# Condition and bias products moved, transposes at two maxima, last block in chunks, warm rows removed: an adaptive-norm, attention and quantized FFN kernel

## The reference, cut to what matters

```python
def _L0_cond_ref(Efou, y, weight):
    w = scale * weight[:, :, :, 0] * y[:, None, :]
    w = w * jax.lax.rsqrt(jnp.sum(w * w, axis=2, keepdims=True) + 1e-08)
    ...
def _L0_ffn_ref(x, weight, aux_weight1, aux_weight2, bias):
    return jnp.tanh(((x @ weight) @ aux_weight1) @ aux_weight2 + bias)
def _L1_cond_ref(X1, X2, Wq1, bq1, Wq2, bq2, Wk1, bk1, Wk2, bk2, Wv, bv, alpha):
    Q1 = X1e @ Wq1 + bq1; K1 = X1e @ Wk1 + bk1       # X1e: the condition, the same for every token
    Q2 = X2 @ Wq2 + bq2;  K2 = X2 @ Wk2 + bk2
    A = softmax(Q2 K2^T * s) - alpha * softmax(Q1 K1^T * s)
    return A @ (concat(X1e, X2) @ Wv + bv)
def _L1_ffn_ref(x, clip_x, clip_down, w_gate, w_up, w_down):
    xq = _act_fake_quant(x, clip_x[0])               # scale from max(abs(x)) over the tensor
    h = _act_fake_quant(silu(xq @ q(w_gate).T) * (xq @ q(w_up).T), clip_down[0])
    return h @ q(w_down).T
x = x + _L0_ffn_ref(_L0_cond_ref(x, cond, ...), ...)
x = x + _L1_ffn_ref(_L1_cond_ref(cond, x, ...), ...)
```

## Time and profile before

| | |
|---|---|
| median of 3 runs | 229.44 us (228.91 to 229.47) |
| the profiled execution | 227.23 us |
| its span, first to last instruction | 225.4 us |
| granted PE clock, mean | 0.995 of full |
| busy: PE / DVE / ACT / POOL | 214.4 / 161.2 / 121.3 / 109.3 us |
| the chain that ended last | PE 86%, DVE 9%, POOL 1%, ACT 1%, issue 1% |

### The profile page before, as it was taken

One profiled execution on the slowest core, in us unless ns is written; L12 is line 12 of the kernel. 1 busy time (PEld: TensorE's weight loads), 2 busy tenths in 40 slices (PEclk: granted clock), 3 DMA queues, 4 the chain that ended last, 5 costly groups with the idle time before them and its releaser, 6 DMA issues.

```text
span 225.4 us, 4018 instructions
## 1 busy us (share of the span) xinstructions
PE 214.4 (95%) x1556; PEld 185.9 (82%) x1559; DVE 161.2 (71%) x327; ACT 121.3 (54%) x203; POOL 109.3 (48%) x126
## 2 busy tenths in 40 slices
PE   6799999999999999999999999999999899998991
PEld 5699899889999999999999999999999444452480
DVE  1634435899488569688696876958676879998964
ACT  3447824655044919144181541906329889885870
POOL 8240841244000626229377383784951145683782
PEclk9999999999999999999999999999999999999998
DMA  6980008500000000000000000000000000000045
GB/s 188 330 319 7 0 3 236 174 0 3 0 0 3 0 0 3 0 3 1 1 3 0 0 3 0 0 3 0 3 0 0 1 3 1 0 3 0 0 164 208
DMA packets 6970, 9.37 MB, mean 42 GB/s; under 512 B 788, under 2 KB 4904, under 8 KB 6952
## 3 DMA queue, kind: packets, MB, share of 16 engines
q1 hardware_dynamic: 6480, 8.85, 11.6%
q10 hardware_dynamic: 152, 0.26, 0.3%
q0 software_dynamic: 320, 0.01, 0.1%
HBM read 7.02 MB, written 2.10 MB: 40 GB/s over the span
## 4 chain that ended last, share of the span: by engine, by line
PE 86%; DVE 9%; POOL 1%; issue 1%; ACT 1%; POOLq 0%; DVEq 0%
PE ps L1137 57%; PE ps L1509 8%; PE ps L1351 3%; PE ps L1121 2%; PE ps L1592 2%; PE ps L1403 2%; DVE hmax L935 2%; PE ps L1170 1%; PE ps L1575 1%; DVE downT L786 1%; PE ps L1188 1%; PE ps L1316 1%; DVE hi L996 1%; PE ps L1210 1%; PE ps L1614 1%
## 5 line engine op out<-in xcount | busy, mean ns | idle before, releaser
L505 ACT ACTIVATE prob<-prob 128x512 f32<-128x512 f32 x32 | 19.8, 620 | 35.5 <-DVE prob L809 35.5
L1070 POOL TENSOR_TENSOR ptl<-prob,pth 128x512 fp32r<-128x512 f32 x16 | 20.3, 1295 | 37.9 <-ACT pth L417 37.9
L1137 PE MATMUL ps<-xh,x1h 128*128 128x256 f32 x128 | 37.2, 290 | 0.0
L1137 PE MATMUL ps<-xh,x1l 128*128 128x256 f32 x128 | 36.1, 282 | 0.0
L1137 PE MATMUL ps<-xl,x1h 128*128 128x256 f32 x128 | 36.1, 282 | 0.0
L1137 PE MATMUL ps<-vh,ptl 128*128 128x258 f32 x112 | 31.7, 283 | 0.0
L786 DVE TENSOR_REDUCE downT<-ps 128x256 f32<-128x1024 f32 x16 | 19.5, 1217 | 12.3 <-PE ps L1137 12.2
L1070 POOL TENSOR_TENSOR ptl<-prob,xh 128x512 fp32r<-128x512 f32 x13 | 16.5, 1296 | 17.8 <-ACT xh L417 17.8
L1137 PEld LDWEIGHTS ps<-xh,x1h 128*128 128x128 f32 x128 | 24.4, 190 | 0.2
L1137 PEld LDWEIGHTS ps<-xl,x1h 128*128 128x128 f32 x128 | 24.4, 191 | 0.0
L1137 PEld LDWEIGHTS ps<-xh,x1l 128*128 128x128 f32 x128 | 24.4, 191 | 0.0
(11 more groups left out here) (264 smaller groups left out, 616.2 us busy)
## 6 DMA issues: line engine op xcount, KB each, us to landing
result<-yst SPq DMA_DIRECT2D x8, 256.0 KB, 2.1
xn<-in_x SPq DMA_DIRECT2D x2, 512.0 KB, 9.4
xn<-in_x SPq DMA_DIRECT2D x3, 256.0 KB, 5.6
wdn<-in_L_ffn_w_down SPq DMA_DIRECT2D x1, 704.0 KB, 6.9
wgn<-in_L_ffn_w_gate SPq DMA_DIRECT2D x1, 640.0 KB, 4.5
wun<-in_L_ffn_w_up SPq DMA_DIRECT2D x1, 640.0 KB, 5.2
a<-in_L_ffn_aux_weight SPq DMA_DIRECT2D x2, 256.0 KB, 5.1
wvf<-in_L_cond_Wv SPq DMA_DIRECT2D x1, 512.0 KB, 11.1
```

The source lines that it names most:

```text
L505: act.activation(prob[:, 2 * k:2 * k + 2, :], prob[:, 2 * k:2 * k + 2, :], ACT.Exp, scale=ATT_SCALE).then_inc(p_ready, 1)
L1070: pool.tensor_tensor(ptl[:, g % 2, 2 * k:2 * k + 2, :], prob[:, 2 * k:2 * k + 2, :], pth[g % 2][:, 2 * k:2 * k + 2, :].bitcast(F32), ALU.s ...
L1137: last = pe.matmul(dst, a, b, start=(n == 0), stop=(n == len(passes) - 1))
```

## The change

- The condition's products with Wq1 and Wk1 are made at the start, around `scaled_T(0)`, from `ycol` into bank 1; wq1 and wk1 are loaded ahead of wf, and a2 after the second half of x. DVE copies the eight results; the second half of `mix(0)` waits for that copy.
- The bias products are made by DVE, four multiply-and-sum operations on wk2s and wq2s with the biases loaded to all partitions; SP waits for them before it loads the FFN weights. The three sums over partitions become one of four columns. `warm(WARM2)` is gone, DVE's Newton step is an operation shorter, and `scaled_T` signals each half.
- `up` 1 moves to the end of the attention in the place of `down` 0; both `down` transposes move behind L1558, at the second maximum, with their own banks and ACT copies.
- All `keep_warm` calls are gone.
- x's first piece is widened by DVE right after its rounding (before: after one rounding more); piece (1, 1) by DVE where POOL did it. The first hidden piece (0, 0) is widened by DVE right after its rounding where POOL did it.
- In the last block half oc = 0 is made as a whole, then oc = 1 in two chunks of 256 columns in banks of their own, each scaled and added by DVE in PSUM and stored by itself (128 KB).

```diff
-    after_attend = {4: ("gate", 0), 5: ("gate", 1), 6: ("up", 0), 7: ("up", 1)}
+    after_attend = {4: ("gate", 0), 5: ("gate", 1), 6: ("up", 0)}
...
-    at_end = [("out", NP - 2), ("tile", 0), ("down", 0), ("tile", 1), ("down", 1)]
+    at_end = [("out", NP - 2), ("tile", 0), ("up", 1), ("tile", 1)]
...
-    pieces = [(0, 0, "dve", "pool"), (0, 1, "act", "act"), (0, 2, "dve", "pool"), (0, 3, "dve", "pool"),
+    pieces = [(0, 0, "dve", "dve"), (0, 1, "act", "act"), (0, 2, "dve", "pool"), (0, 3, "dve", "pool"),
...
+            sp.dma_start(wq1s[:], square(wq1)).then_inc(ld_q1, 16)
+            sp.dma_start(wk1s[:], square(wk1)).then_inc(ld_k1, 16)
             sp.dma_start(wf[:], square(l0_w)).then_inc(ld_wf, 16)
             sp.dma_start(a1[:], square(l0_a1)).then_inc(ld_a1, 16)
-            sp.dma_start(a2[:], square(l0_a2)).then_inc(ld_a2, 16)
             for c in range(DC):
                 sp.dma_start(xn[:, 0, c, half(1)], x_rows(0, c)[:, half(1)]).then_inc(ld_x0[1][c], 16)
+            sp.dma_start(a2[:], square(l0_a2)).then_inc(ld_a2, 16)
...
-            sp.dma_start(wq1s[:], square(wq1)).then_inc(ld_q1, 16)
-            sp.dma_start(wk1s[:], square(wk1)).then_inc(ld_q1, 16)
+            sp.wait_ge(yT_raw_ps, 1)
+            for row, v in ((bq2_row, bq2), (bk2_row, bk2)):
+                sp.dma_start(row, v.rearrange("(a d) -> a d", a=1).broadcast_to([P, D])).then_inc(ld_bias_rows, 16)
...
+            sp.wait_ge(uw_ready, 2 * DC)
...
+            for k in range(2):
+                sp.wait_ge(added["dve"], k + 1)
+                sp.dma_start(rows_of[DC - 1][:, (q0 + k) * D:(q0 + k + 1) * D],
+                             yst[:, NH - 1, DC - 1, k * D:(k + 1) * D]).then_inc(stored, 16)
...
             def mixT_hi(b):
-                act.wait_ge(wT_ps, b + 1)
                 act.wait_ge(ycol_ready, 1)
                 for i in range(DC):
+                    act.wait_ge(wT_ps, b * DC + i + 1)
...
+            for c in range(DC):
+                act.wait_ge(downT_ps, c + 1)
+                copy(downT[:, :, c * P:(c + 1) * P],
+                     ps[:, down_bank[c], :].bitcast(BF16)[:, 0:IC * P].rearrange("p (i n) -> p i n", i=IC), downT_ready)
...
+            for name, w, row in (("ucol", wk2s, bq2_row), ("wbcol", wq2s, bk2_row)):
+                for c in range(DC):
+                    dve.scalar_tensor_tensor(out=junk_row, in0=w[:, c, :], scalar=1.0, in1=row, op0=ALU.mult,
+                                             op1=ALU.mult, accum_out=col(name, c)).then_inc(uw_ready, 1)
+                    dve.wait_ge(uw_ready, (name == "wbcol") * DC + c + 1)
...
             x_round(0, 0)
+            x_widen(0, 0, 1)
             x_round(1, 0)
-            dve.wait_ge(xi_dve, 1)
-            dve.tensor_copy(x_piece(xq, 0, 0), x_piece(xi, 0, 0)).then_inc(xq_dve, 1)
             x_round(1, 1)
             dve.tensor_scalar(gus[:], wsc[:, 0:12], col("sx"), None, ALU.mult).then_inc(scales_ready, 1)
+            x_widen(1, 1, 3)
...
+            def scaled_last(oc, k):
+                n, s = NH - 1, slice(k * D, (k + 1) * D)
+                dve.wait_ge(rows_ps, (NH - 1 - ROWS) * DC + 1 + k + 1)
+                at_bank = ps[:, last_bank[k], 0:D]
+                dve.scalar_tensor_tensor(out=at_bank, in0=at_bank, scalar=col("hs"), in1=wbc[:, k, :], op0=ALU.mult,
+                                         op1=ALU.mult).then_inc(last_scaled, 1)
+                dve.wait_ge(last_scaled, k + 1)
+                dve.tensor_tensor(yst[:, n, oc, s], at_bank, yst[:, n, oc, s], ALU.add).then_inc(added["dve"], 1)
...
-            warm(WARM2)
...
+            pe.wait_ge(ycol_ready, 1)
+            pe.wait_ge(ld_q1, 16)
+            cond_vectors(0, wq1s)
             scaled_T(0)
+            pe.wait_ge(ld_k1, 16)
+            cond_vectors(4, wk1s).then_inc(vec_ps, 1)
...
-            bias_vector(0, wkT, C_BQ2)
             square_mm(6, wqT, wkT).then_inc(g_ps, 1)
-            bias_vector(2, wqT, C_BK2)
-            mix(2, {0: lambda: cond_vectors(4, wq1s), 1: lambda: cond_vectors(8, wk1s).then_inc(vec_ps, 1)})
+            mix(2)
...
-            pe.wait_ge(vec_ready, 4)
-            for k in range(DC):
-                pe.matmul(ps[:, 7, 16:18], ones[:], col("prod", 2 * k, 2), start=(k == 0), stop=(k == DC - 1))
-            pe.matmul(ps[:, 7, 18:20], ones[:], col("bb", 0, 2), start=True, stop=True).then_inc(a1dot_ps, 1)
+            pe.wait_ge(vec_ready, 2)
+            pe.matmul(ps[:, 7, 16:20], ones[:], col("pz", 0, 4), start=True, stop=True).then_inc(a1dot_ps, 1)
...
             spread_max(col("am"), AMAX_BANK).then_inc(amT_ps, 1)
-            do_extra(at_end[-1])
-            keep_warm(0, 5)
...
-            keep_warm(WARM_BANK, 10)
+            down_weight_T(0)
+            pe.wait_ge(x1n_ready, 3)
+            down_weight_T(1)
+
+            pe.wait_ge(downT_ready, 1)
             pe.wait_ge(hm_ready, NMAX + 1)
             spread_max(col("hm"), HMAX_BANK).then_inc(hmT_ps, 1)
-            keep_warm(WARM_BANK, 8)
...
+                if n == NH - 1:
+                    for oc in range(DC):
+                        pe.wait_ge(yT_ready, (n - 2) * DC + oc + 1)
+                        if oc == 0:
+                            for i in range(IC):
+                                piece_ready(i)
+                                rows(i, oc)
+                            continue
+                        pe.wait_ge(y_ready, DC)
+                        for k in range(2):
+                            for i in range(IC):
+                                last = row_product(i, oc, k, i == 0, i == IF, ps[:, last_bank[k], 0:D])
+                            last.then_inc(rows_ps, 1)
+                    return
```

More of the change, by code:

```diff
@@ L83, in build_block @@
     POOL_UNITS = [2, 4, 6, 8, 9]
-    WARM0, WARM1, WARM2 = 9, 4, 5
+    WARM0, WARM1 = 9, 4
     AHEAD = 1
@@ L247, in build_block @@
         MISC, MAXB = 7, 6
-        own_bank = {("out", NP - 2): 2, ("tile", 0): 3, ("tile", 1): MAXB, ("down", 0): 4, ("down", 1): 5}
+        own_bank = {("out", NP - 2): 2, ("tile", 0): 3, ("tile", 1): MAXB, ("up", 1): 4}
+        down_bank = (5, 4)
+        last_bank = (3, 4)
         def o_bank(g, t):
@@ L397, in _ @@
                 b, q0 = n // 2, 2 * (n % 2)
+                rows_of = out[b].rearrange("(c p q) f -> c p (q f)", p=P, q=NQ)
                 for oc in range(DC):
+                    if (n, oc) == (NH - 1, DC - 1):
+                        break
                     if n < ROWS:
@@ L531, in extra_read @@
                     kind, c = item
[L532 to L538 removed]
+                    act.activation((gateT if kind == "gate" else upT)[:, c, :], src[:, 0:I],
+                                   ACT.Copy).then_inc(misc_used, 1)
             for v in range(NT):
@@ L559, in _ @@
             act.activation(col("junk"), ones[:, 0:1], ACT.Silu)
-            for item in at_end[1:-1]:
+            for item in at_end[1:]:
                 extra_read(item)
@@ L976, in down_out, with scaled @@
                                              op0=ALU.mult, op1=ALU.add).then_inc(yT_ready, 1)
-            def scaled(n):
-                for oc in range(DC):
+            def scaled(n, ocs=range(DC)):
+                for oc in ocs:
                     dve.wait_ge(rows_ps, (n - ROWS) * DC + oc + 1)
@@ L984, in scaled, with widen @@
                                              op1=ALU.mult).then_inc(scaled_ready, 1)
-                for oc in range(DC):
-                    if add_on(n, oc) == "dve":
-                        dve.wait_ge(scaled_ready, (n - ROWS) * DC + oc + 1)
-                        dve.tensor_tensor(yst[:, n, oc, :], x1T[:, n, oc, :], yst[:, n, oc, :],
-                                          ALU.add).then_inc(added["dve"], 1)
+            def widen(q):
+                dve.wait_ge(rounded[q[2]], rounded_upto(q, q[2]))
+                dve.tensor_copy(piece_of(hq, hqr, q), piece_of(hi8, hir, q)).then_inc(hq_ready["dve"], 1)
             dve.wait_ge(wbc_ready, 2)
@@ L997, in _ @@
                                           ALU.mult).then_inc(rounded["dve"], 1)
-                for q in pieces:
+                    if q == pieces[0] and n == 0:
+                        widen(q)
+                for q in pieces[1:]:
                     if q[0] == n and q[3] == "dve":
-                        dve.wait_ge(rounded[q[2]], rounded_upto(q, q[2]))
-                        dve.tensor_copy(piece_of(hq, hqr, q), piece_of(hi8, hir, q)).then_inc(hq_ready["dve"], 1)
+                        widen(q)
                 if n == 0:
@@ L1211, in scaled_T, with cond_vectors @@
                                          diag[:, b, o, :], start=True, stop=True)
-                last.then_inc(wT_ps, 1)
+                    last.then_inc(wT_ps, 1)
+            def cond_vectors(at_col, w):
+                for m in range(DC):
+                    for k in range(DC):
+                        last = pe.matmul(ps[:, 1, at_col + 2 * m:at_col + 2 * m + 2], w[:, k, m * P:(m + 1) * P],
```

(23 more changed lines are left out.)

118 lines of the change are left out of this document (62 added, 56 removed), and 2 rows, old and new, of the table at.

## The result

| | before | changed |
|---|---|---|
| median of 4 runs | 229.30 us (228.91 to 229.47) | 231.72 us (230.23 to 232.87) |
| ratio | | 1.0124, interval 1.0082 to 1.0165 |
| the profiled execution | 227.23 us, span 225.4 | 232.87 us, span 231.1 |
| granted clock, mean | 0.995 | 0.980 |

The account below looks back on a forecast made before the run. PE was taken as the bound, busy 214.4 of 225.4 us. Terms -0.5 - 1.9 - 0.5 + 0.3 - 1.0, warm rows 0, gave -3.6 from 229.44: 225.8 us, own range 224.9 to 226.8, with rivals 224.6 to 228.6.

Parts of the forecast that it names:

- Part 6: Warm rows removed at both maxima: frees no chain, PE's rests of 2.2 and 3.8 us keep the clock; 0 us.
- rival A: Clock falls before the down projections at the second maximum: +0.6 to +1.8 us, about 227.0 us; chance 0.17.
- Rivals A and B: Beside rival A, B: clock falls at the first maximum or both, slowing the FFN; 227.5 to 228.7 us, chance 0.12.
- Part 1: Start: first mix begins earlier because DVE's wTl comes sooner, PE having nearly no slack; about -0.5 us (-0.6 to 0).
- Part 2: Main stretch: 3.5 us of PE products removed, less stalls of 0.9 and 0.7; about -1.9 us (-2.3 to -1.1).
- The two stalls: PE waits 0.9 us for POOL before the third mix and 0.7 for DVE's sums before the dot product.
- Part 3: First maximum: transposes moved, DVE makes POOL's late cast for the FFN's second half; about -0.5 us (-0.9 to 0).
- Part 4: Second maximum: first cast moves to DVE, down(0) starts earlier and down(1) later; about +0.3 us (-0.1 to +0.45).
- the port rule of the Trainium skill: Second maximum: DVE and GpSimd share a port pair exclusively, so DVE's cast costs POOL too; +0.6 us, sum -3.3.
- Part 5: Last block: one half finished early, the other in two chunks, three stores; about -1.0 us (-1.4 to -0.6).
- rival D: Slower than before: clock falls at the first maximum and stays low well into the FFN; 10 us give 230.8, chance 0.07.

Follow-up runs that it names:

- g4: f4 without the seven unread matmuls at the first maximum; median 228.76 us, ratio 1.0029 to the kernel before.
- h1: The changed kernel run again without edit, on another chip; median 233.34 us against 227.54 for the kernel before, executions 224.7 to 234.2.
- f2: The kernel before without its 23 unread matmuls at the two maxima; median 230.45 us (4 executions), ratio 1.0107.
- g3: f4 timed again as a control; median 226.33 us, ratio 0.9935 to the kernel before.
- e4: The changed kernel with the early warm transposes and the unread matmuls at both maxima put back; median 225.97 us, ratio 0.9917 to the kernel before.
- f1: The kernel before without the five early warm transposes after the norms; median 229.63 us against 227.43, ratio 1.0067.
- e3: The changed kernel with only the unread matmuls at both maxima put back; median 227.54 us, ratio 0.9918 to the kernel before.
- g2: f4 with the first hidden piece cast on POOL again, as before the change; median 226.27 us, ratio 0.9926 to the kernel before.
- f3: The kernel before with only the last block in the new order; median 227.94 us, ratio 0.9981.
- f4: The changed kernel with all warm rows put back and condition products and their loads where they were; median 225.40 us, ratio 0.9911 to the kernel before.

## Why the prediction was wrong, point by point

**Part 6, warm rows: 0. This step failed.** The sum had nothing for the clock. In the changed kernel's first profile it took 8.2 us: 6.4 in the start, 1.7 in the FFN, 0.1 after it (0.4 up to down(1), of which 0.3 came back by the end). For the maxima, I took the only fall of the trace, 2.9 us after PE's last matmul, as the measure of a rest that PE may take, and judged 2.2 us safe. One fall, from a PE that never worked again, is no bound from below. At the first maximum 2.4 us of rest cost about 1.65 us in g4 and 1.7 in the changed kernel's first profile, but 2.8 in h1's, where the low level lasted twice as long. At the second, down(1) began 0.4 later in the changed kernel, hidden in part by the casts, as rival A argued, and 1.6 later in f2. Rivals A and B named the mechanism of this part, and most of these prices lie near theirs (1.65 at the first maximum, 0.6 to 1.8 at the second). Their chances, 0.17 and 0.12, were too low: the fall is nearly the rule. The sentence from the Trainium skill ("TensorE: Matmul & The Clock Gate", "HAM oscillation — how this bites in real kernels") that speaks against the change was the better guide. Its example has pauses of about 3 to 5 us; the traces agree with it for one of 2.4 us too, at 184.5 us, and at 211.8 us.

**Part 1, start: -0.5. The sum was right only at full pace, and the price of the removed rows was missing.** g3 has the first mix at 10.82, 0.52 earlier than before, with the warm transposes kept and without the moved products. With these products e4 has it at 11.35: PE's queue was as full as I feared, and 0.5 was gone. What no rival of mine held is the clock in the start. PE begins at half pace in every profile here. I read it in the earlier trace rows, priced it as a pace, and then used the five warm transposes as free PE time. f1 shows their worth by themselves: 1 to 2 us. In the changed kernel's first profile the low pace lasted to 20.5 us. Then the two-column products, cheap at full pace, took 1.50 instead of 0.79 and stood in front of the first mix. The same page of the Trainium skill says in its "Part 1" that the slow state is the default and that activity releases the gate; the start of every profile here agrees. h1's shows that activity did not keep the gate open there: the clock fell again at 8.9 us with PE at work. Why a given launch rises late, or rises and falls again, is not settled. Nor do the runs tell whether the moved products have a part in it or only stand, at half pace, in front of the first mix. Without the early transposes the executions spread over 2.8 us where the products stay (f1) and over 6.6 where they are moved (e3), but the two kernels differ in more than that.

**Part 2, products: -1.9.** Measured -1.56 (e4, from the first to the fourth mix). The two stalls came where they were put: 1.13 before the third mix, where POOL's low half is done at 28.0 (0.9 forecast), and a wait of PE of 0.8 ahead of the dot product at 35.67, for DVE's last small operation (0.7 forecast). The remainder is in the small DVE work with its waits (34.34 to 35.63, 1.29 against 1.05) and the one dot product, 0.39 against 0.22.

**Part 3, first maximum: -0.5.** -0.26: the FFN's second half gave -0.38, where -0.37 was worked out, the removal of up(1) in front of the last block gave nothing, and DVE's last scaled output waited 0.16 more.

**Part 4, second maximum: +0.3.** +0.19 in e4; by g2 against g3 0.11 of it is the cast. The rows were nearer than the estimate of +0.6 by the port rule of the Trainium skill ("SBUF — State Buffer", "SBUF: two separate sides").

**Part 5, last block: -1.0.** -0.87, in two ways. PE needed 0.4 longer for the last block than before (3.30 against 2.89), but DVE and the stores gained more.

**Sum.** Without the clock -2.5 instead of -3.6 in e4, or about -2.8 by its fastest execution with the warm transposes gone (e3's 224.40 against 227.22). So the range would have held a kernel that kept its warm rows. That e4's median, 225.97, stands beside the 225.8 of the forecast is luck: the base, 229.44, was 2.0 above the 227.46 of the kernel before beside e4, and the gain of 3.6 was 2.1 above the 1.5 between the medians there. The base was the median of three executions, all of the slower group of the kernel before (228.9 to 229.5), and the 2.2 us above the profiled one, which I took for independent of the change, come from the start, by the profiles of f2, f3 and f4. Only the outcome of rival D, slower than before, is what happened. Its mechanism was one long fall in the FFN; the first profile shows a late start and two falls of 3.4 us, h1's a fall in the start, one of 6.8 us at the first maximum and a short one.

## What to carry to other kernels

Matmuls that nobody reads may carry more than they cost. Before taking them out, add up at which pace the work behind them runs if the clock falls once, and count a rest of PE like the 2.4 us here, ahead of PE-bound work, as a fall, not as a small risk. Filler belongs in the waits. Useful products in front of a cold start are a bet: they bought 0.7 us in the best executions here and stand on the chain at half pace in the worst. And with executions that fall in groups, compare group with group: one profile shows one group, and a part worth 0.9 us can vanish in a ratio of medians.

## What the runs showed of the hardware that was not expected

- In the changed kernel's first profile the granted clock is shown as 1.00 over the whole start, while its 24 matmuls took 5.40 us there and 3.13 later. In f1's and h1's a low stretch is shown there, from 9.1 to 16.0 and from 8.9 to 15.7, behind a stretch at full pace. So in the start the clock row shows a fall, but not that the pace has not risen yet; that has to be read from the durations of like instructions.
- In h1 the clock fell in the start without a wait of PE before it; in f1 behind a wait of 1.0 us.
- A rest of 2.4 us (g4, the changed kernel) was enough for a fall to 0.50; one of 1.6 (f2, first maximum) brought none. In the changed kernel's first profile each low stretch at the maxima lasted about 3.4 us (184.5 to 187.9, 211.8 to 215.2), although PE was in steady work in the first; in h1's the first one lasted 6.8 (179.6 to 186.4).
- In f2 the low stretch at the second maximum, with PE waiting between casts, lasted from 205.9 to about 212.6, twice as long.
- The same program varies by 10 us between launches on one chip (h1, 224.7 to 234.2), and the differences that the profiles show between e4 and the changed kernel are of when the clock rises and falls; most executions have no profile.
